# Reordered instruction lists in an attention and mixture-of-experts kernel: low weights last, a matmul quarter ahead of the transposes, two lists swapped, two sums moved

## The reference

```python
kv = k_v @ W_k.T + b_k
out = jnp.einsum('bij,bjd->bid', p, kv)             # p = layernorm(x)
sim = jnp.einsum('bid,bjd->bij', out, kv) * scale   # then layernorm over j, gamma, beta
x = x + softmax(sim)
...
gate = jnp.einsum('btd,edf->ebtf', layernorm(x), Wg)     # + x Ga Gb for experts 0 and 1
up = jnp.einsum('btd,edf->ebtf', layernorm(x), Wu)       # + x Ua Ub for experts 0 and 1
mid = jax.nn.silu(gate) * up
out = jnp.einsum('ebtf,efd->ebtd', mid, Wd)              # + mid Da Db for experts 0 and 1
x = x + jnp.einsum('bte,ebtd->btd', router_weights, out)
```

## Time and profile before

| | |
|---|---|
| median of 3 runs | 1043.31 us (1042.74 to 1044.19) |
| the profiled execution | 1044.28 us, its span 1042.5 us |
| PE busy | 1029.0 us, 99% of the span |
| PEld / DVE / ACT / POOL busy | 841.7 / 751.0 / 457.8 / 80.3 us |
| granted TensorE clock | 1.00 throughout |
| chain that ended last | PE 83%, DVE 9%, DMA 2%, ACT 2%, issue 2% |

### The profile page before, as it was taken

The page is one execution under the profiler, slowest core; times in us unless marked ns, Lnnn a source line. Parts: engine busy times, 40 slices in busy tenths (PEclk is TensorE's granted clock), DMA queues, the critical chain, the costliest instruction groups (busy, mean ns, idle before and its releaser), DMA issues.

```text
span 1042.5 us, 12575 instructions
## 1 busy us (share of the span) xinstructions
PE 1029.0 (99%) x4641; PEld 841.7 (81%) x4641; DVE 751.0 (72%) x1268; ACT 457.8 (44%) x708; POOL 80.3 (8%) x113
## 2 busy tenths in 40 slices
PE   7999999999999999999999999999999999999998
PEld 5887877878888888888888788888888888888886
DVE  6878678967484765758566695886868586977664
ACT  4664363563353343425434344453635263534530
POOL 2511121100001000000100011000000000000000
PEclk9999999999999999999999999999999999999999
DMA  9410104249557483855748674525343544444342
GB/s 297 161 51 1 81 21 162 76 112 297 201 194 269 141 275 132 281 194 196 265 132 289 206 254 120 183 96 219 118 172 103 212 131 165 159 162 162 106 177 81
DMA packets 95709, 173.43 MB, mean 166 GB/s; under 512 B 5728, under 2 KB 62240, under 8 KB 94752
## 3 DMA queue, kind: packets, MB, share of 16 engines
q1 hardware_dynamic: 87584, 125.37, 36.8%
q0 software_dynamic: 7776, 47.19, 12.2%
q10 hardware_dynamic: 288, 0.07, 0.0%
HBM read 111.23 MB, written 61.37 MB: 166 GB/s over the span
## 4 chain that ended last, share of the span: by engine, by line
PE 83%; DVE 9%; DMA 2%; ACT 2%; issue 2%; SPq 0%; POOL 0%; DVEq 0%
PE gate_up L2045 15%; PE gate_up L2047 15%; PE gate_up L2046 15%; PE tiles L1931 6%; PE tiles L1933 6%; PE tiles L1932 6%; PE tiles L2065 4%; PE tiles L2064 4%; PE tiles L2063 4%; PE gate_up L2002 2%; PE gate_up L2003 2%; PE gate_up L2008 2%; DVE piece_lo L1422 1%; PE tiles L1967 1%; DMA wd_raw<-in_wd_dram 1%
## 5 line engine op out<-in xcount | busy, mean ns | idle before, releaser
L2045 PE MATMUL gate_up<-xT_hi,piece_hi 128*128 128x512 f32 x448 | 175.0, 391 | 0.5 <-DVE mids L1463 0.3
L2047 PE MATMUL gate_up<-xT_lo,piece_hi 128*128 128x512 f32 x448 | 174.4, 389 | 0.0
L2046 PE MATMUL gate_up<-xT_hi,piece_lo 128*128 128x512 f32 x448 | 174.3, 389 | 0.0
L2045 PE MATMUL gate_up<-tx_hi,piece_hi 128*128 128x512 f32 x336 | 131.1, 390 | 1.6 <-DVE gates L1451 1.6
L2046 PE MATMUL gate_up<-tx_hi,piece_lo 128*128 128x512 f32 x336 | 130.8, 389 | 0.0
L2047 PE MATMUL gate_up<-tx_lo,piece_hi 128*128 128x512 f32 x336 | 130.8, 389 | 0.0
L1422 DVE TENSOR_TENSOR piece_lo<-piece,piece_hi 128x1024 fp32r<-128x1024 f32 x88 | 93.1, 1099 | 29.0 <-ACT piece_hi L956 28.4
L969 ACT ACTIVATE gate_up<-gate_up 128x512 f32<-128x512 f32 x56 | 32.6, 582 | 182.7 <-PE gate_up L2047 122.1
L1931 PE MATMUL tiles<-wd_hi,mids_hi 128*128 128x512 f32 x256 | 99.7, 390 | 0.4 <-DVE mids_lo L1504 0.4
L2045 PEld LDWEIGHTS gate_up<-xT_hi,piece_hi 128*128 128x128 f32 x448 | 84.1, 188 | 19.5 <-issue 0.7
L1933 PE MATMUL tiles<-wd_hi,mids_lo 128*128 128x512 f32 x256 | 99.6, 389 | 0.0
(11 more groups left out here) (214 smaller groups left out, 1914.9 us busy)
## 6 DMA issues: line engine op xcount, KB each, us to landing
piece_spill<-piece_hi POOLq DMA_DIRECT2D x24, 896.0 KB, 4.6
piece_spill<-piece_lo POOLq DMA_DIRECT2D x24, 896.0 KB, 6.8
piece_hi<-piece_spill SPq DMA_DIRECT2D x24, 896.0 KB, 4.5
piece_lo<-piece_spill SPq DMA_DIRECT2D x24, 896.0 KB, 6.4
piece<-in_wg_dram SPq DMA_DIRECT2D x24, 256.0 KB, 4.3
piece<-in_wu_dram SPq DMA_DIRECT2D x24, 256.0 KB, 6.2
merged<-lora_w SPq DMA_DIRECT2D x6, 1024.0 KB, 6.1
wd_raw<-in_wd_dram SPq DMA_DIRECT2D x5, 1024.0 KB, 5.3
```

What stands on the lines that cost most here:

```text
L2045: nc.tensor.matmul(dst, w_h, x_h, start=first and kt == 0, stop=False, skip_group_check=True)
L2046: nc.tensor.matmul(dst, w_l, x_h, start=False, stop=False, skip_group_check=True)
L2047: ins = nc.tensor.matmul(dst, w_h, x_l, start=False, stop=last and kt == 1, skip_group_check=True)
```

## The change

Five edits, all of order:

1. In units 1 to 3 of the first half block, the low weights (POOL and DVE make them) are multiplied last, and PE waits for them only there. Unit 0 is as before. The transposes of the second pair of row tiles, ahead of unit 3, come before its wait for low weights.
2. In `first_expert(0, ...)` the third down quarter stands ahead of block 1's transposes, and on ACT the first `normalise` ahead of the last high part of `mid`.
3. In step 0: `wd_low_part` behind the closing gate combination and the next piece's sums; on ACT `copy_p5(3)` ahead of the high part of piece 4; `make_mid(0, 0, C21)` ahead of a low part, the low part of piece 4 and `add_lora`.
4. In step 6 the first two back sums stand behind `combine(6, GATE, 1, C22)`, no longer ahead of `add_down(5, 0)`.
5. In step 7 the last `mid_low_part` goes ahead of the swap's second low part.

```diff
-            for f in range(FT):
-                if f < 3:
-                    pe.wait_ge(w_gu_ready, f + 1)
-                if f >= 2:
-                    pe.wait_ge(w_rest_ready, f - 1)
+            pe.wait_ge(w_gu_ready, 1)
+            unit(FIRST_HALF, 0, 0, FIRST, 2)
+            for f in range(1, FT):
                 if f == FT - 1:
                     for t in PAIRS[1]:
                         pe.wait_ge(sim_read, t + 1)
                         transpose_x2(0, t, tiles[:, SIM_BANK[t], :])
-                unit(FIRST_HALF, 0, f, FIRST, 2 if f == 0 else None)
+                first_half_unit(f)
...
+            def first_half_unit(f):
+                pe.wait_ge(mid_made, FIRST_HALF * FT + f - 1 + EARLIER + UNIT_CREDIT)
+                pe.wait_ge(w_hi_made, f + 1)
...
+                for m in range(2):
+                    dst = gate_up[:, 2 * p + m, FIRST]
+                    for k in range(KT):
+                        nc.tensor.matmul(dst, w_hi[:, m, k, cols], x_hi[:, k, FIRST], start=(k == 0), stop=False)
+                        nc.tensor.matmul(dst, w_hi[:, m, k, cols], x_lo[:, k, FIRST], start=False, stop=False)
+                if f < 3:
+                    pe.wait_ge(w_gu_ready, f + 1)
+                if f >= 2:
+                    pe.wait_ge(w_rest_ready, f - 1)
+                for m in range(2):
+                    for k in range(KT):
+                        ins = nc.tensor.matmul(gate_up[:, 2 * p + m, FIRST], w_lo[:, m, k, cols], x_hi[:, k, FIRST],
+                                               start=False, stop=(k == KT - 1))
...
                 down(n, 0)
                 down(n, 1)
+                if tokens == SECOND:
+                    down(n, 2)
                 pe.wait_ge(mid_made, a * FT + EARLIER + UNIT_CREDIT)
                 for t in range(TT):
                     transpose_x2(a, t, gate_up[:, t, :])
-                down(n, 2)
+                if tokens == WHOLE:
+                    down(n, 2)
                 down(n, 3)
...
+                if tokens == SECOND:
+                    unit_silu(n, 3, tokens)
+                    normalise(n + 1, 0, more, n + 3)
+                    unit_high_part(n, 3, tokens)
...
                 if k == 0:
+                    copy_p5(j + 3)
                     piece_high_part(j + 4)
-                mid_high_part(k, 0, C22)
-                copy_p5(j + 3)
+                    mid_high_part(k, 0, C22)
...
                     t_low_part(5, tx_lo[:, 1, :], x_back[:, 1, :], tx_hi[:, 1, :])
+                    mid_low_part(k - 1, 1, C21)
                     t_low_part(6, tx_lo[:, 2, :], x_back[:, 3, :], tx_hi[:, 2, :])
-                    mid_low_part(k - 1, 1, C21)
...
                     combine(k, GATE, 1, C12)
-                    wd_low_part(k)
                     combine(k, GATE, 1, C22)
                     piece_sums(j + 3)
+                    wd_low_part(k)
...
-                    if k == SWAP - 1:
-                        back_sum(0, 1, 4)
-                        back_sum(2, 3, 4)
                     add_down(k - 1, 0)
...
                     combine(k, GATE, 1, C22)
                     if k == SWAP - 1:
+                        back_sum(0, 1, 4)
+                        back_sum(2, 3, 4)
                         back_sum(1, 3, 6)
...
                 make_mid(k, 0, C22)
+                if k == 0:
+                    make_mid(k, 0, C21)
                 mid_low_part(k, 0, C11)
```

More of the change, by code:

```diff
@@ L800, in unit, with unit_silu @@
             def unit(n, f, tokens=WHOLE):
+                unit_silu(n, f, tokens)
+                unit_high_part(n, f, tokens)
+            def unit_silu(n, f, tokens):
                 u = n * FT + f + EARLIER
@@ L805, in unit, with unit_high_part @@
                   .then_inc(silu_made, 1)
-                act.wait_ge(mid_made, u + 1 + UNIT_CREDIT)
+            def unit_high_part(n, f, tokens):
+                act.wait_ge(mid_made, n * FT + f + EARLIER + 1 + UNIT_CREDIT)
                 if tokens == WHOLE:
@@ L930, in first_expert @@
                 unit(n, 2, tokens)
-                unit(n, 3, tokens)
-                for t in range(TT):
+                if tokens == SECOND:
+                    unit_silu(n, 3, tokens)
+                    normalise(n + 1, 0, more, n + 3)
+                    unit_high_part(n, 3, tokens)
+                else:
+                    unit(n, 3, tokens)
+                    normalise(n + 1, 0, more, n + 3)
+                for t in range(1, TT):
                     normalise(n + 1, t, more, n + 3)
@@ L1835, in _ @@
                     add_lora(k)
-                make_mid(k, 0, C21)
+                if k != 0:
+                    make_mid(k, 0, C21)
                 combine(k, UP, 1, C12)
@@ L1989, in logits @@
                 ins.then_inc(logits_mm, 1)
+            def first_half_unit(f):
+                pe.wait_ge(mid_made, FIRST_HALF * FT + f - 1 + EARLIER + UNIT_CREDIT)
+                pe.wait_ge(w_hi_made, f + 1)
+                p = f % 2
+                cols = slice(f * P, (f + 1) * P)
+                x_hi, x_lo = block_of(xT_hi, 0), block_of(xT_lo, 0)
+                for m in range(2):
[11 more added lines that the diff above has]
+                                               start=False, stop=(k == KT - 1))
+                ins.then_inc(gu_mm, 1)
             def unit(n, b, f, tokens=WHOLE, tiles_made=None):
```

## The result

The changed kernel takes 1045.25 us (median of 14 runs, 1044.30 to 1047.16), the kernel before 1043.54 (14 runs, 1042.74 to 1044.35). The ratio is 1.0019, 95% interval [1.0011, 1.0026]: 1.7 us slower by the medians and 2.0 by the ratio, where 1.3 were forecast. The interval leaves out 1, so the loss is real, though its middle lies just inside the 0.2% that the prediction took for the smallest change that can be told. The profiled execution took 1046.19 us (span 1044.5).

What follows compares the result with a forecast made beforehand. PE, busy 99% of the span, bounds the kernel, with DVE's list next; 0 + 0.4 - 1.15 + 2.0 = +1.3 us on the median of 1043.31 gives 1044.6 us, range 1041.6 to 1047.0.

Steps and rivals of the forecast that it cites:

- Edit 1, forecast 0: First half block: PE's 0.8 us of waits for low weights go, but are spent waiting for ACT's scaled rows: 0.
- Edit 2, forecast +0.4: Block 1: PE gains 1.5 us at the transposes, loses it waiting some 2 us for DVE at the logits: +0.4 us.
- Edit 3, forecast -1.15: Step 0: the wait at 219.41 and two smaller ones go; product 4 starts 1.3 us earlier, 0.15 lost again: -1.15 us.
- Edits 4 and 5, forecast +2.0: Steps 6 and 7: two PE waits go, but late reloads delay the fourth back sum by 2.8 us: +2.0 us.
- -0.76: Steps 6 and 7: PE's change in us up to the last down quarter at 618.97, before the reloads' delay is added.
- the formula: Steps 6 and 7: cost is -0.76 us plus a delay of 2t - 9.2 us, t being a reload pair's time.
- The chain: Steps 6 and 7: later back sums, then reloads, fourth sum 2.8 us late, then DVE and ACT, then PE in quad 27.
- B: Steps 6 and 7: the second reload pair takes 8 us, delay 4.8, sum +3.3: 1046.6 us; chance 0.27.
- C: Steps 6 and 7: a reload pair is complete in 4.6 us, delay 0, sum -1.5: 1041.8 us; chance 0.12.
- D: All edits: nothing comes late, DVE makes room everywhere, every wait is a gain, 6.1 us: 1037.2 us; chance 0.06.

## Why the prediction was right

The forecast was 1044.6 us and no change beyond what can be told; measured 1045.25. Of the 0.65 us between them, 0.23 are the base, since the kernel before has a median of 1043.54 over 14 runs and not 1043.31. That it stayed within 0.2% was close: the ratio is 1.0019 and its interval reaches 1.0026. Step by step:

- Edit 1, forecast 0 with a wait of about 0.9 us for ACT: the wait is 0.7, the gain 0 by the marks, 0.9996 alone. Right.
- Edit 2, forecast +0.4: PE's own gain of 1.5 us is there (transposes of 1.91 us, the stream 1.4 us ahead of before), DVE is late at the logits, PE waits 1.85 us, and the logits come 0.55 us later. The mechanism is as predicted. What the step left out is what follows the wait: where it says "its own 1.5 us lost in a wait of some 2 us", it takes the wait for the whole price. In 5 of 14 executions the lower clock adds to it, 1.66 us in the profiled one, 1.1 us between the medians (1046.19 against 1045.09), 1.4 to 1.9 in edit 2 alone. On an average over executions this term should have been about +1, not +0.4, and this is the mis-sized one: at full clock the changed kernel's median of 1045.09 lies 1.55 above before, close to the +1.3.
- Edit 3, forecast -1.15: -1.19 by the marks (0.92 at the first wait, the rest by quad 5), -1.1 by the medians alone. Product 4 of quad 3 came with a first matmul of 0.50 us after it, the small loss that was foreseen.
- Edits 4 and 5, forecast +2.0 with the pair's time t = 6.0 twice. The pairs took 6.4 and 6.0, so the delay is 12.4 - 9.2 = 3.2, and with -0.76 the formula gives +2.4; the marks give +2.47 in the changed kernel and +2.19 alone, where the pairs took 6.4 and 5.8 (formula: 2.2). The chain was right link by link, PE's waits at quad 27 too; the cost was 0.2 to 0.5 us above the forecast, the first pair's extra 0.4 us.
- The rivals. B, slow reloads, needs a mean of 6.4; it was 6.2, so the truth lies between the forecast and B. C, quick reloads, falls: no pair with all its bytes that was timed took under 5.8. By the Trainium skill (DMA: Bandwidth & Descriptors, section "Anatomy of one DMA — SWDGE (gpsimd) path") a pair would be estimated at 4.4 us, but its fit was measured on transfers that GpSimd issues, and SyncE issues these. The traces have 5.8 to 6.4, and 5.0 with half the bytes, so the fit does not carry over, mostly in its fixed part. D falls with three new waits of PE.

In the one pair of profiles the account is +3.5 us and not +1.3. Of these 2.2 us, 1.7 are the clock, 0.5 the reloads and 0.15 the logits. That the medians came out so near the forecast is in part luck: most executions of the changed kernel kept their clock.

The forecast was made against one profiled execution and then moved down by the 0.97 us that this one lay above the median of three. A late start is at least a part of these: its first transposes stand at 24.07. In the nine kernels without the wait at the logits, the six profiled executions with that mark at 23.18 to 23.75 lie within 0.3 us of the median of their runs, the three at 24.24, 24.34 and 24.52 lie 0.6, 1.3 and 2.2 above it. Without that step the forecast would have been 1045.6.

What stays open: why the clock falls in some executions and not in others after the same wait of 1.85 us (0.998 in 18 of 47). The executions differ in when PE gets there, by up to 1.8 us of their start among other things. Of the four profiles with this wait, the two whose clock fell started earliest (first transposes at 22.73 and 23.02), the two that kept it later (23.24 and 23.55); four are too few, and no run varied that alone.

## What to carry to other kernels

When the engine that bounds a kernel waits for a list of another engine, ask of each instruction ahead in that list what hangs on it: move the one whose result is needed last (here a low part that was done at 580.7, even behind the combination, and first read at about 597.6), not the one at the head of a chain of transfers. A matmul engine that is brought forward into a result that cannot come earlier gains nothing and may lose its clock; give the supplier the same lead, or leave it. And read a change part by part at marks that both traces share: a sum of -1.2, 0, about +1 and +2.4 showed as "about the same".

## What the runs showed of the hardware

- After 1.85 us without matmuls, in a stream otherwise dense for tens of us, TensorE's granted clock fell to 0.50 (1.2 GHz) in two of the four profiles that have this wait. Read in stretches of 0.5 us, it fell 1.2 and 1.5 us after the matmuls had begun again and stayed low for about 3.4 us. By the mean clock it did so in 18 of 47 executions, at a price of 1.1 to 1.9 us. With the wait filled by matmuls, none of 11 showed it.
- Other waits brought no lower clock: 1.54 and 1.57 us in quad 27 of the changed kernel, 3 us of matmuls apart (1.00 from 560 to 640), 1.3 and 1.6 us at the same two places with edits 4 and 5 alone (none of 11 executions), and 1.80 us at 18 to 20 us in the profile before, where PE is less densely busy (1.00 there).
- A pair of 512 KB transfers from DRAM, issued by SyncE 0.4 us apart, took 5.8 to 6.4 us from the first issue to the reader's start; with half the bytes 5.0. The landing of the first fell from 4.5 to 3.4 us after its issue, of the second from 5.4 to 4.6.
- Fourteen profiled executions, of kernels that are the same up to there, differ by up to 1.8 us within the first 25 us. For effects of 1 us, two single profiles have to be aligned behind that.
